# Inverse square roots by an element-wise power on GpSimd in a chain of eight sublayers

## What is computed

```python
x = L0_attn_a_up_x
x = x + _L0_attn_a_ref(_layernorm(x), ...)   # "mamba": selective scan
x = x + _L0_ffn_ref(_layernorm(x), ...)      # "local0": six layers of local attention and FFN
x = x + _L0_attn_b_ref(_layernorm(x), ...)   # "dense_attn"
x = x + _L0_ffn_ref(_layernorm(x), ...)      # "local1"
x = x + _L1_attn_a_ref(_layernorm(x), ...)   # "linear_attn"
x = x + _L1_ffn_ref(_layernorm(x), ...)      # "fp4_0"
x = x + _L1_attn_b_ref(_layernorm(x), ...)   # "head_attn"
x = x + _L1_ffn_ref(_layernorm(x), ...)      # "fp4_1"
```

```python
def _layernorm(x, axis=-1, eps=1e-05):
    m = jnp.mean(x, axis=axis, keepdims=True)
    v = jnp.var(x, axis=axis, keepdims=True)
    return (x - m) / jnp.sqrt(v + eps)
...
def l2norm(t):      # queries and keys of each of 16 heads, in each of the six layers of _L0_ffn_ref
    return t / jnp.maximum(jnp.linalg.norm(t, axis=-1, keepdims=True), 1e-12)
```

## Time and profile before

| | |
|---|---|
| median of 3 runs | 4342.93 us (4341.33 to 4343.28) |
| span of the profiled execution | 4339.8 us |
| what lies around the span, against the median | 3.1 us |
| mean granted TensorE clock | 0.957 of full speed |
| busy, share of the span | PE 92%, DVE 86%, ACT 78%, POOL 78% |
| the two `local` sublayers | 488 to 2145 us and 2288 to 3942 us, 76% of the span |

### The profile page before, as it was taken

One profiled execution on the slowest core, in us unless ns is written; L12 is line 12 of the kernel. 1 busy time (PEld: TensorE's weight loads), 2 busy tenths in 40 slices (PEclk: granted clock), 3 DMA queues, 4 the chain that ended last, 5 costly groups with the idle time before them and its releaser, 6 DMA issues. The chain is left out here.

```text
span 4339.8 us, 130231 instructions
## 1 busy us (share of the span) xinstructions
PE 3995.2 (92%) x46283; PEld 2655.5 (61%) x46283; DVE 3715.0 (86%) x12505; ACT 3380.3 (78%) x10657; POOL 3380.2 (78%) x4196
## 2 busy tenths in 40 slices
PE   6888799999999999999767999999999999996686
PEld 2333357767767767766553677767776776763464
DVE  6999789999999999999476999999999999974646
ACT  5888489999999999999414999999999999983122
POOL 3999698888888888888296888888888888861313
PEclk7999899999999999999897999999999999997887
DMA  1000101111111111111002111111111111100000
GB/s 28 1 1 1 46 24 31 41 31 36 41 27 49 31 34 44 26 34 27 15 1 53 31 27 41 36 41 31 36 41 27 51 29 29 37 24 3 6 3 10
DMA packets 78571, 122.04 MB, mean 28 GB/s; under 512 B 26024, under 2 KB 47204, under 8 KB 77924
## 3 DMA queue, kind: packets, MB, share of 16 engines
q1 hardware_dynamic: 77924, 113.71, 10.3%
HBM read 35.56 MB, written 1.05 MB: 8 GB/s over the span
## 5 line engine op out<-in xcount | busy, mean ns | idle before, releaser
L1095 POOL TENSOR_TENSOR local_qk<-local_qk,local_rb 128x512 f32<-128x512 f32 x768 | 975.7, 1271 | 224.2 <-DVE local_rb L1485 210.1
L1365 ACT ACTIVATE local_pr<-local_tb,local_nmax 128x96 f32<-128x96 f32 x3072 | 995.0, 362 | 68.7 <-DVE local_nmax L1501 67.1
L1191 PE MATMUL local_pj<-local_wqkv,local_xs 128*128 128x512 f32 x1536 | 808.4, 619 | 31.8 <-DVE local_rb L1485 17.8
L1101 POOL TENSOR_TENSOR local_qk<-local_qk,local_rinv 128x512 f32<-128x512 f32 x768 | 786.6, 1045 | 7.5
L1501 DVE CUSTOM_DVE_ANT_0 local_tb<-local_tb,local_mask 128x96 f32<-128x96 f32 x3072 | 689.2, 290 | 46.5 <-PE local_tb L1213 43.7
L1365 ACT ACTIVATION_READ_ACCUMULATOR local_pr<-local_tb,local_nmax 128x1 f32 x3072 | 703.3, 229 | 0.0
L1117 POOL TENSOR_TENSOR local_pr<-local_pr,local_rsum 128x384 f32<-128x384 f32 x768 | 622.4, 826 | 36.5 <-DVE local_rsum L1507 36.5
L1482 DVE TENSOR_TENSOR local_qk<-local_pj,local_rope 128x512 f32<-128x512 f32 x768 | 523.6, 682 | 62.8 <-ACT local_sq L1348 44.1
L1348 ACT ACTIVATE local_sq<-local_pj 128x512 f32<-128x512 f32 x768 | 462.2, 627 | 123.3 <-PE local_pj L1191 119.0
L1485 DVE TENSOR_TENSOR local_rb<-local_pj,local_rope 128x512 f32<-128x512 f32 x768 | 523.2, 681 | 2.8 <-POOL local_qk L1095 2.8
L1492 DVE TENSOR_REDUCE local_ss<-local_sq 128x8 f32<-128x512 f32 x768 | 512.0, 678 | 2.6 <-ACT local_sq L1348 0.8
(11 more groups left out here) (425 smaller groups left out, 7954.8 us busy)
## 6 DMA issues: line engine op xcount, KB each, us to landing
local_v<-local_v SPq DMA_DIRECT2D x288, 256.0 KB, 3.9
local_wqkv<-L_ffn_Wqkv_dram SPq DMA_DIRECT2D x72, 256.0 KB, 4.7
local_wo<-L_ffn_Wo_dram SPq DMA_DIRECT2D x12, 512.0 KB, 4.0
local_w<-L_ffn_W_dram SPq DMA_DIRECT2D x12, 341.0 KB, 4.8
mamba_parts<-mamba_in_low SPq DMA_DIRECT2D x24, 64.0 KB, 2.0
local_w<-L_ffn_W_dram SPq DMA_DIRECT2D x12, 128.0 KB
y_dram<-store_xtok SPq DMA_DIRECT2D x4, 256.0 KB, 2.9
local_oT<-rope_dram SPq DMA_DIRECT2D x2, 256.0 KB, 2.7
```

The costliest lines, as they stand in the source:

```text
L1095: nc.gpsimd.tensor_tensor(qk[:, u, :], qk[:, u, :], rb[:, u % 2, :], ALU.add).then_inc(s["summed"], 1)
L1101: nc.gpsimd.tensor_tensor(heads8(qk[:, u, :]), heads8(qk[:, u, :]), r, ALU.mult).then_inc(s["scaled"], 1)
L1191: nc.tensor.matmul(bank[:, :], xs[:, par, u // 4 * P:(u // 4 + 1) * P], wqkv[:, dep % 2, u % 4 * BANK:(u % 4 + 1) * BANK], start=True, sto ...
L1365: ins = nc.scalar.activation(pr[:, (NU * c + k) % PR_RING, i, WIN:WIN + KW], scores[:, i * KW:(i + 1) * KW], ACT.Exp, scale=-1.0, bias=nma ...
```

## The change

Three things are done.

1. `root` in `local_transformer` becomes two steps: the clamp, as before, and one `tensor_tensor` of GpSimd with the operation `pow`, clamped sums to the power of a constant tile `minus_half`, 128 x 64. The tiles of the rounds go.
2. In `normalise`, DVE only adds epsilon. GpSimd then takes the power of the 16 variances of each partition in one instruction, behind what `beside_pool` gave it. PE waits for GpSimd (`rooted`) in place of DVE. One tile of roots is cleared and not two.
3. GpSimd fills `minus_half` once, while x is loaded.

```diff
@@ load_stream, gpsimd
             nc.gpsimd.memset(net.ones[:, :], 1.0)
+            nc.gpsimd.memset(net.minus_half[:, :], -0.5)
@@ normalise, gpsimd
-            for r in root:
-                nc.gpsimd.memset(r[:, :], 0.0).then_inc(cleared, 1)
+            nc.gpsimd.memset(root[:, :], 0.0).then_inc(cleared, 1)
             for sem in net.past:
                 pool.sem_clear(sem)
             if beside_pool:
                 beside_pool(pool)
+            pool.wait_ge(cleared, 1)
+            pool.wait_ge(with_eps, 1)
+            nc.gpsimd.tensor_tensor(by_tile(root[:, :]), var[:, :, :], view(net.minus_half[:, 0:1], [[NT, NC], [1, NT]]), ALU.pow).then_inc(rooted, 1)
@@ normalise, tensor
-            pe.wait_ge(roots, 1 + ROOT_STEPS)
-            nc.tensor.transpose(p_rootT, root[1][:, :], net.ident[:, :]).then_inc(turned, 1)
+            pe.wait_ge(rooted, 1)
+            nc.tensor.transpose(p_rootT, root[:, :], net.ident[:, :]).then_inc(turned, 1)
@@ normalise, vector
-            nc.vector.tensor_scalar(var[:, :, :], by_tile(p_var), LN_EPS, None, ALU.add).then_inc(roots, 1)
-            dve.wait_ge(cleared, 2)
-            dve.wait_ge(roots, 1)
-            inverse_root(nc, dve, roots, 1, var[:, :, :], [by_tile(r[:, :]) for r in root], [t[:, :, :] for t in tmp])
+            nc.vector.tensor_scalar(var[:, :, :], by_tile(p_var), LN_EPS, None, ALU.add).then_inc(with_eps, 1)
@@ local_transformer, gpsimd
-POOL_STEPS = 1 + 3 * 4
+ROOT_ALL = 2
...
             def root(a, par, step):
-                x, y, t = ssc[:, :], (root0[:, :], rinv[:, :]), [r[:, :] for r in rt]
                 if step == 0:
                     pool.wait_ge(s["summed_sq"], QK_UNITS * a + QK_UNITS)
                     need(pool, s["scaled"], QK_UNITS * a)
-                    nc.gpsimd.tensor_scalar(x, ss[:, par, :], 1e-24, None, ALU.max).then_inc(s["root_steps"], 1)
+                    nc.gpsimd.tensor_scalar(ssc[:, :], ss[:, par, :], 1e-24, None, ALU.max).then_inc(s["root_steps"], 1)
                 else:
                     pool.wait_ge(s["root_steps"], ROOT_ALL * a + step)
-                    pool_root_step(nc, step - 1, x, y, t).then_inc(s["root_steps"], 1)
+                    nc.gpsimd.tensor_tensor(rinv[:, :], ssc[:, :], net.minus_half[:, :], ALU.pow).then_inc(s["root_steps"], 1)
...
                 run(root, 0, 0)
                 run(root, 0, 1)
-                run(root, 0, 2)
...
-                run(root, 0, 13)
                 run(scale, 0, 0)
```

More of the change, by code:

```diff
@@ L79, in __init__ @@
         self.ones = root.sb("ones", [P, P])
+        self.minus_half = root.sb("minus_half", [P, P // 2])
         self.pick = root.sb("pick", [P, BANK // P, P])
@@ L180 @@
 SEED = float(0x5F3759DF)
[L181 to L224, removed]
 def warm(nc, net, bank, count):
@@ L247, in normalise @@
         var = m.sb("var", [P, NC, NT])
-        root = [m.sb(f"root{i}", [P, P]) for i in range(2)]
-        tmp = [m.sb(f"tmp{i}", [P, NC, NT]) for i in range(2)]
+        root = m.sb("root", [P, P])
         rootT = m.sb("rootT", [P, P])
@@ L253, in normalise @@
         p_var, p_rootT, p_idle = p_bc[:, NC - 1, 0:P], p_bc[:, NC - 2, 0:P], p_bc[:, 0, :]
-        cleared, centred, squared, summed, roots, turned, copied, spread = (
-            net.sem(f"{tag}_ln_{n}") for n in ("cleared", "centred", "squared", "summed", "roots", "turned", "copied", "spread"))
+        cleared, centred, squared, summed, with_eps, rooted, turned, copied, spread = (
+            net.sem(f"{tag}_ln_{n}") for n in ("cleared", "centred", "squared", "summed", "with_eps", "rooted", "turned", "copied", "spread"))
         x = net.xT[:, :, :].rearrange("p b l -> p (b l)")
@@ L966, in local_transformer @@
         ssc = m.sb("ssc", [P, 2 * 2 * HEADS])
-        root0 = m.sb("root0", [P, 2 * 2 * HEADS])
         rinv = m.sb("rinv", [P, 2 * 2 * HEADS])
-        rt = [m.sb(f"rt{i}", [P, 2 * 2 * HEADS]) for i in range(2)]
         rb = m.sb("rb", [P, 2, BANK])
@@ L1037, in couple @@
             return kk // 2, kk % 2
-        ROOT_ALL = 1 + POOL_STEPS
         @block.sync
@@ L1139, in iteration @@
                 run(root, 0, 1)
-                run(root, 0, 2)
[L1141 to L1147, removed]
-                run(root, 0, 10)
-                run(root, 0, 11)
-                run(root, 0, 12)
-                run(root, 0, 13)
                 run(scale, 0, 0)
```

## The result

The changed kernel took 4956.82 us (median of 4 runs, 4953.5 to 4957.76); the kernel before, beside it, 4342.13 us. The ratio is 1.1418 [1.1402, 1.1434], a loss of 615 us. The forecast was 4342.2 us, and the range ended at 4500: it was wrong, and the case that came was rival A.

The account below looks back on a forecast made before the run. Four well-filled engines bound the local sublayers, with GpSimd least loaded and nobody waiting for it in steady iterations. -1.5 - 2.2 + 3.0 = -0.7 us gave a span of 4339.1, plus 3.1 around it: 4342.2 us; range 4330 to 4500.

Parts of the forecast that it names:

- rival A: PE's transpose of units 0 and 1, each iteration: long power makes GpSimd the bound; D = 8 some 4490 us; chance 0.27.
- the room: Local sublayers: GpSimd's first pair of scales ends 1.79 us before PE transposes those units, so a longer chain is hidden.
- the cliff at D = 6.5: Steady local iterations: above 6.5 us the power is no longer covered and PE waits, each us costing 94 iterations.
- D: Time of one 128x64 power on GpSimd, replacing 13 instructions of 4.92 us; taken as 4 us, bounds 0.3 and 11.
- The rule by the Trainium skill: Price of the power at the plain 2.12 ns per column: D a little over 6.6 us, on the edge of its cover.
- The first iterations: First iteration of each local sublayer, where PE waits 2.17 us for the first scales: 0.75 us shorter twice, -1.5 us.
- The normalisations: Eight, with a 16-column power of 1.14 us: three gated by DVE -2.2, three by warming matmuls 0, two before locals +3.0.
- rival C: Normalisations: a 16-column power has a high fixed price, 3 us per call whatever its width; +11 us, 4354; chance 0.04.
- Rival B: Local iterations: relief on GpSimd shortens each by 0.2 us, through something the waits do not show; -19 us, 4323; chance 0.10.

Follow-up runs that it names:

- the kernel with 48 columns: The changed kernel with the power on 48 of 64 columns, the other 16 roots left out and kept at one: 4808.27 us, ratio 1.1063.

## Why the prediction was wrong, step by step

**What bounds the kernel, and the room.** Right. The room of 1.79 us and the cliff at D = 6.5 came from two timelines of the kernel before, and three runs stand on it: 5.46 us on the power left the iteration at 32.65, 8.05 us made it 34.31, and 10.58 us with the clock held made it 37.07. PE's waits of 1.59 and 4.11 us are what the room gives (1.51 and 4.04) within 0.1.

**The step that failed is D.** The prediction took 4 us, on the ground that operations inside one instruction write nothing back between them. It is 10.58. What lies inside the instruction no run shows; measured is that a power costs 160 ns per column, and a product 2.12: 75 times as much, where I had assumed some 40 products and then gone below that. The upper end of 11 us, a mere doubling, held the true value, and so did the width of the doubt; but the value taken leaned on the lower rows, and the 0.27 for rival A was too little for a cost that the trace did not show. With bounds of 0.3 and 11 and a cliff at 6.5, the two sides are by their width near a coin's toss, not 2 to 1 for the near side. The rule by the Trainium skill (GPSIMD Engine Reference, Performance pitfalls for Q7 kernels), priced at 6.6 us, stood on the right side of the cliff, by 0.1 us; measured is 4 us more. By that page's 4 cycles at 1.2 GHz the 160 ns per column would be, as an estimate, 48 links instead of the 30 I had assumed.

**Rival A had the right place and too low a price.** Its own sum at D = 10.58 is 94 x 4.04 + 7 = 387, some 4729 us; measured are 4956.8. What it left out is the clock, a term that the prediction's sum does not have at all. PE's wait of 4 us is followed by matmuls at the lower of its two levels (1.2 instead of 2.4 GHz, granted clock 0.50: the projection in 3.78 us where 1.99 is the time at full clock), and this costs some 2 us more in each iteration. The account now:

| term | us |
|---|---|
| 96 x (10.58 - 6.54), the wait itself | 388 |
| 96 x 2.2, PE at the lower level behind the wait | 211 |
| the normalisations, measured alone | 5 |
| sum | 604 |
| measured | 615 |

The 2.2 is 38.9 - 36.69, read from iterations; 1.8 of it came back when the wait was filled. That the level falls because PE stands still is shown by that run. The two profiles give the same split without the model: PE's idle time ahead of the transposes grew from 11.1 to 413.0 us, by 402, and its busy time, with the same matmuls, from 3995.2 to 4200.6, by 205. That is 607 of the 616 us between the spans; the other 9 are idle time of PE elsewhere, the normalisations among it.

**The first iterations.** Predicted 1.5 us shorter. PE's first transpose waits 7.54 us for GpSimd in local0 where it waited 2.17:

```profile
540.21 1.12 PE L1189 MATMUL local_tb<-net_ident,local_qk 64*128 64x64 f32 x16 [7.54 <-POOL local_qk L1054]
```

That is 5.4 us longer (5.8 in local1), near the 10.58 - 4.75 = 5.8 by which the chain grew.

**The normalisations.** Predicted +0.8 us in sum, measured +5 [2, 10]. The power of 16 columns takes 2.91 us, not 1.14. These rows answer to the earlier trace rows:

```profile
4669.51 0.17 DVE L279 TENSOR_SCALAR fp_ln_var<-fp_ln_p_bc 128x16 f32<-128x16 f32 x1 [7.88 <-PE fp_ln_p_bc L243]
4669.84 2.91 POOL L232 TENSOR_TENSOR fp_ln_root<-fp_ln_var,net_minus_half 128x16 f32<-128x16 f32 x1 [7.74 <-DVE fp_ln_var L279]
4672.80 0.18 PEld L255 LDWEIGHTS fp_ln_p_bc<-net_ident,fp_ln_root 128*128 128x128 f32 x1 [0.80 <-POOL fp_ln_root L232]
```

Epsilon to weight load is 3.29 us in place of 2.38, as rival C's sum had it (a call of 3 us), so its +11 is near the 10.5 us to which the eight stretches from epsilon to load add up in the profile, though the kernel with this part alone lost 5 by its median. But its reason is wrong: the fixed part is 0.36 us, and the price is the columns. In the dense_attn block it is 3.29 against 2.77. Ahead of local0 the power does queue behind the tables as predicted, and PE's load is released by GpSimd:

```profile
498.29 2.90 POOL L232 TENSOR_TENSOR local_ln_root<-local_ln_var,net_minus_half 128x16 f32<-128x16 f32 x1
501.25 0.18 PEld L255 LDWEIGHTS local_ln_p_bc<-net_ident,local_ln_root 128*128 128x128 f32 x1 [4.90 <-POOL local_ln_root L232]
```

**Rival B** (a relief that shortens the iteration) never had its condition: there was no relief.

What stays open: why the lower clock lasts longer in some iterations than in others behind the same wait (38.2 to 39.8 us), and what holds VectorE's seed through five of GpSimd's instructions in one iteration and through one in another. Whether VectorE would take the same power cheaply was not tried on the chip.

## What to carry to other kernels

One instruction is not cheaper than thirteen because it is one: for a function whose price no row shows, time it first in a quiet stretch of the kernel, at the shape in question. Where a cliff lies inside the bounds of an unknown cost, the forecast is a weighing of the two sides of the cliff, not of the middle of the bounds. And an engine that nobody waits for has exactly its slack to give; beyond it each microsecond is paid once as a wait and again through TensorE's clock (here 2.2 us on a wait of 4.1, but some 0.2 on one of 1.6), and moving the step about on the engine helps only down to the engine's own sum of work.

## What the runs showed of the hardware that was not expected

- A power on GpSimd costs about 0.36 us and 160 ns per column, the same for 16, 64 and 128 partitions and for exponents of 2 and -0.5. A product of 64 columns costs 0.31 us, a power 10.55.
- A `tensor_scalar` of VectorE on 128 x 4 numbers, SBUF to SBUF, took 4.60 us while GpSimd worked through five instructions without a gap, and 0.16 us when it read PSUM; this edit alone was worth 267 us in the kernel with 48 columns, and nothing in the kernels before and after, where it had taken 0.44 and 0.41 us. The Trainium skill (SBUF — State Buffer, Who interferes with whom) says that VectorE and GpSimd share a port pair under an exclusive lock. The trace agrees in that at least 90 of 96 seeds end with a GpSimd instruction, and it shows more: a row of GpSimd's instructions can keep VectorE out through five of them, not only the one beside which VectorE came. That it is this lock that holds the seed is inferred from these ends and from the run with PSUM, not read from a row.
- The clock costs after a short wait: 4.11 us idle, and at a granted clock of 0.50 the transposes take 1.12 us instead of 0.71 and the 8 matmuls behind them 3.78 instead of 1.99. After 1.59 us idle it fell in one iteration of ten only. Twenty useless matmuls in the wait, 4.49 us of them, made the kernel 175 us faster than the changed one (the other edit in it, the seed from PSUM, was worth nothing by itself; without it the same matmuls made the kernel some 160 us slower).
